# Openings of two large attentions reordered, and the second router moved into its layer norm

## What is computed

```python
x = L0_attn_a(x)   # two-way Mamba
x = L0_ffn(x)      # depthwise conv, 8 experts, top 2
x = L0_attn_b(x)   # linear recurrence
x = L0_ffn(x)
x = L1_attn_a(x)   # 16 heads of 8, local window 128, plus 64-token latent attention, gated mix
x = L1_ffn(x)      # second layer norm, router, 8 experts, top 2, plus a shared expert
x = L1_attn_b(x)   # 16 heads of 8, rotary positions, causal
x = L1_ffn(x)
```

## Time and profile before

| | |
|---|---|
| median of 3 runs | 6284.84 us (6282.61 to 6287.77) |
| profiled execution, time | 6280.3 us |
| profiled execution, span | 6278.3 us |
| PE busy | 5075.5 us (81%) |
| DVE busy | 4231.9 us (67%) |
| POOL busy | 3279.0 us (52%) |
| ACT busy | 3138.2 us (50%) |
| mean granted clock of PE | 0.899 |

### The profile page before, as it was taken

The page is one execution under the profiler, slowest core; times in us unless marked ns, Lnnn a source line. Parts: engine busy times, 40 slices in busy tenths (PEclk is TensorE's granted clock), DMA queues, the critical chain, the costliest instruction groups (busy, mean ns, idle before and its releaser), DMA issues. The chain is left out here.

```text
span 6278.3 us, 78842 instructions
## 1 busy us (share of the span) xinstructions
PE 5075.5 (81%) x21870; PEld 2565.6 (41%) x21934; DVE 4231.9 (67%) x6079; ACT 3138.2 (50%) x5353; POOL 3279.0 (52%) x2351
## 2 busy tenths in 40 slices
PE   4888888888887797778977999854897799964897
PEld 1333333333332343534433555422565344432664
DVE  4889889999988474044765888752675566652675
ACT  4656656655654454223544777721232477731232
POOL 2888888888886252012623444317333456527333
PEclk8999999999999897578988999966998899976998
DMA  1233322222221000000001333222454343302455
GB/s 71 83 118 135 127 75 89 82 75 88 82 75 67 0 0 0 0 0 0 0 6 47 91 87 88 53 82 74 154 189 153 75 95 97 90 1 76 160 188 173
DMA packets 203166, 494.21 MB, mean 79 GB/s; under 512 B 32448, under 2 KB 57664, under 8 KB 191424
## 3 DMA queue, kind: packets, MB, share of 16 engines
q1 hardware_dynamic: 184640, 452.25, 23.0%
q0 software_dynamic: 18176, 37.79, 1.7%
HBM read 381.79 MB, written 108.12 MB: 78 GB/s over the span
## 5 line engine op out<-in xcount | busy, mean ns | idle before, releaser
L360 POOL TENSOR_TENSOR mamba_bu<-mamba_du,mamba_b_all 128x1024 f32<-128x1024 f32 x512 | 1197.3, 2355 | 229.7 <-PE psum L454 172.3
L636 DVE TENSOR_TENSOR_SCAN mamba_bu<-psum,mamba_bu 128x512 f32<-128x512 f32 x1024 | 1189.6, 1205 | 132.7 <-POOL mamba_bu L360 88.6
L454 PE MATMUL psum<-mamba_bu,consts 128*128 128x512 f32 x2048 | 976.4, 600 | 6.1 <-DVE mamba_bu L642 1.5
L568 ACT ACTIVATE psum<-mamba_delta,A 128x510 f32<-128x510 f32 x1024 | 690.8, 685 | 545.8 <-DVE mamba_bu L636 524.2
L1754 ACT ACTIVATE ffn_moe_act<-ffn_moe_act 128x512 f32<-128x512 f32 x344 | 216.9, 631 | 721.2 <-DVE ffn_moe_act L1798 721.1
L642 DVE TENSOR_TENSOR mamba_bu<-mamba_bu,psum 128x1024 f32<-128x1024 f32 x448 | 536.8, 1198 | 58.4 <-remote 51.5
L1639 POOL DMA_INDIRECT results<-ffn_moe_y_rows,ffn_moe_row_of x312 | 302.2, 969 | 506.9 <-DVE ffn_moe_y_rows L1829 431.4
L454 PEld LDWEIGHTS psum<-mamba_bu,consts 128*128 128x128 f32 x2048 | 396.3, 194 | 332.6 <-issue 318.4
L2187 POOL TENSOR_TENSOR loc_q_bd<-loc_q_max,weights_l1a 128x512 fp32r<-128x512 f32 x256 | 274.8, 1103 | 389.6 <-DVE loc_q_max L2431 374.2
L2422 DVE TENSOR_REDUCE cau_top<-psum 128x2 f32<-128x512 f32 (+1 forms) x384 | 263.1, 692 | 181.3 <-PE psum L2254 167.5
L2187 POOL TENSOR_TENSOR cau_q_bd<-cau_q_max,weights_l1b 128x512 fp32r<-128x512 f32 x256 | 258.5, 1044 | 241.2 <-DVE cau_q_max L2431 177.5
(11 more groups left out here) (410 smaller groups left out, 11290.2 us busy)
## 6 DMA issues: line engine op xcount, KB each, us to landing
mamba_b_all<-b_rows SPq DMA_DIRECT2D x256, 512.0 KB
ffn_moe_w_gu<-gate_up_parts SPq DMA_DIRECT2D x78, 1024.0 KB, 4.8
pairs<-empty_rows SPq DMA_DIRECT2D x6, 3432.0 KB, 13.1
ffn_moe_got<-pairs SPq DMA_DIRECT2D x78, 264.0 KB, 3.2
ffn_moe_w_down<-in_l_moe SPq DMA_DIRECT2D x78, 256.0 KB, 2.9
mamba_c_rows<-b_rows SPq DMA_DIRECT2D x32, 512.0 KB, 4.1
qk_rows<-loc_qk SPq DMA_DIRECT2D x16, 1024.0 KB, 7.5
ffn_moe_back<-results SPq DMA_DIRECT2D x32, 512.0 KB, 4.8
```

Of the source, the lines that this page charges most:

```text
L360: nc.gpsimd.tensor_tensor(bu[:, J % BU, :, :], du[:, q % 2, :, :], b, ALU.mult).then_inc(bu_ready, 1)
L454: last = nc.tensor.matmul(ysum[:, h, :], mem.ident, bu[:, J % BU, h, :], start=False, stop=(n == NST - 1), skip_group_check=True)
L568: nc.scalar.activation(by_seq(dA[i % DECAYS])[:, :, 1:S], by_seq(delta[:, q % 2, h, :])[:, :, 1:S], ACT.Exp, scale=mem.A[:, q % 2, h * NST ...
L636: nc.vector.tensor_tensor_scan(bu[:, J % BU, h, :], dA[i % DECAYS], bu[:, J % BU, h, :], 0.0, ALU.mult, ALU.add).then_inc(scanned, 1)
```

## The change

Four things in the attentions. The projections of tile 0 get banks of their own (bank_of: the position of the name in the list of inputs, so banks 0 and 1, or 0 to 3), and only the others claim work. Clearing is moved behind the parts of tile 0 and shared: ACT writes k_st after its two high parts, DVE clears the first k_bd buffer after its work on tile 0, POOL clears the second buffer, top and v after its own. The count is split into four semaphores. The first k_bd buffer is filled by DMAs from ACT's queue, ahead of ACT's high parts of tile 1.

In the norm: a new argument route. With it the loops are written out, PE multiplies U directly by the router's columns (logits), DVE copies the logits out, and l1_router is gone.

```diff
-        (mean_ready, ..., added, scaled) = ctx.enter_context(
+        (mean_ready, ..., added, scaled, shifted, logits_ready, logits_read) = ctx.enter_context(
...
+            def logits(t):
+                pe.wait_ge(shifted, t + 1 + LEAD)
+                pe.wait_ge(logits_read, t - 1 + LEAD)
+                for j in range(SUB):
+                    at = t * T + j * 128
+                    last = nc.tensor.matmul(mem.bank[4 + t % 2][:, j * NE:(j + 1) * NE], dst[:, at:at + 128], route[0], start=True, stop=True)
+                last.then_inc(logits_ready, 1)
+
+            def step(t, s):
+                mean(t + 2, s)
+                var(t, s)
+                if route is not None and t >= 2:
+                    logits(t - 2)
...
+            over_tiles(pe, NT - 2, step)
             var(NT - 2, 0)
             var(NT - 1, 1)
+            if route is not None:
+                for t in range(NT - 4, NT):
+                    logits(t)
...
+            def take_logits(t):
+                dve.wait_ge(logits_ready, t + 1 + LEAD)
+                dve.sem_inc(PASSED[0], 1)
+                nc.vector.tensor_copy(route[1][:, t * SUB:(t + 1) * SUB, :],
+                                      mem.bank[4 + t % 2][:, 0:SUB * NE].rearrange("p (j e) -> p j e", j=SUB)).then_inc(logits_read, 1)
+
+            def step(t, s):
+                center(t + 2, s)
+                scale(t, s)
+                if route is not None and t >= 3:
+                    take_logits(t - 3)
...
             scale(NT - 2, 0)
             scale(NT - 1, 1)
+            if route is not None:
+                for t in range(NT - 5, NT):
+                    take_logits(t)
...
-            l1_router(nc, stage + "_route", mem, U, logits)
...
+        def bank_of(use):
+
+            return mem.bank[inputs.index(use[0])] if use[0] in inputs and use[1] == 0 else work
...
             store_rows(0)
-            sp.wait_ge(zeroed, 6 + LEAD)
+            sp.wait_ge(st_cleared, 1 + LEAD)
             spread_queries(0)
-            spread_diagonal(0)
+            sp.wait_ge(kst_cleared, 2 + LEAD)
             spread_keys(0)
+            sp.wait_ge(bd_cleared, 2 + LEAD)
             spread_diagonal(1)
...
+            def clear_rest():
+                nc.gpsimd.memset(k_bd[:, 1, :, :, :].bitcast(F32), 0.0).then_inc(bd_cleared, 1)
+                nc.gpsimd.memset(top[:, :, :], 0.0).then_inc(cleared, 1)
+                nc.gpsimd.memset(v[:, :, :], 1.0).then_inc(cleared, 1)
...
             def claim(use):
-                pe.wait_ge(work_read, position[use] + LEAD)
+                if bank_of(use) is work:
+                    pe.wait_ge(work_read, position[use] + LEAD)
...
+            high("q", 0)
+            high("k", 0)
             for a in range(2):
-                nc.scalar.activation(k_st[:, a, :, :], ...).then_inc(zeroed, 1)
-            for tile in range(2):
-                high("q", tile)
-                high("k", tile)
+                nc.scalar.activation(k_st[:, a, :, :], ...).then_inc(kst_cleared, 1)
+            act.wait_ge(rows_stored, 16 + LEAD)
+            act.wait_ge(bd_cleared, 2 + LEAD)
+            for i in range(GH):
+                for part in range(PARTS):
...
+                    act.dma_start(k_bd[at:at + HD, 0, :, i, :].bitcast(F32), rows).then_inc(bd_landed[0], 16)
+            high("q", 1)
+            high("k", 1)
...
-            nc.vector.memset(k_bd[:, :, :, :, :].bitcast(F32), 0.0).then_inc(zeroed, 1)
-            if mix is not None:
-                mix.clear(dve)
             for tile in range(2):
...
+                if tile == 0:
+                    nc.vector.memset(k_bd[:, 0, :, :, :].bitcast(F32), 0.0).then_inc(bd_cleared, 1)
+                    if mix is not None:
+                        mix.clear(dve)
-            dve.wait_ge(zeroed, 6 + LEAD)
+            dve.wait_ge(cleared, 2 + LEAD)
             take_v(0)
```

More of the change, by code:

```diff
@@ L58, in tile_pairs, with layer_norm @@
             step(pair * 2 + slot, slot)
-def layer_norm(nc, stage, mem, src, dst, affine=None, twice=False, residual=None):
+def layer_norm(nc, stage, mem, src, dst, affine=None, twice=False, residual=None, route=None):
     with ExitStack() as ctx:
@@ L75, in layer_norm, with over_tiles @@
         ps_var = [mem.bank[2], mem.bank[3]]
-        (mean_ready, centered, squared, var_ready, log_done, rstd_ready, added, scaled) = ctx.enter_context(
-            signals(nc, stage, "mean", "centered", "squared", "var", "log", "rstd", "added", "scaled"))
+        (mean_ready, centered, squared, var_ready, log_done, rstd_ready, added, scaled, shifted, logits_ready, logits_read) = ctx.enter_context(
+            signals(nc, stage, "mean", "centered", "squared", "var", "log", "rstd", "added", "scaled", "shifted", "logits", "logits_read"))
         block = ctx.enter_context(nc.Block())
         n_log = 2 if residual is not None else 1
+        def over_tiles(eng, last, step):
+            if route is None:
+                with eng.Fori(0, last // 2) as pair:
+                    for slot in range(2):
+                        step(pair * 2 + slot, slot)
+            else:
+                for t in range(last):
+                    step(t, t % 2)
         @block.tensor
@@ L139, in square @@
                 nc.gpsimd.tensor_tensor(sq[:, s, :], dst[:, cols(t)], dst[:, cols(t)], ALU.mult).then_inc(squared, 1)
-            tile_pairs(pool, square)
+            over_tiles(pool, NT, square)
         @block.scalar
@@ L1275 @@
 LIMIT = 10.0
[L1278 to L1310, removed]
 BLK = 512
@@ L2189, in diagonal @@
                 last.then_inc(q_bd_ready, 1)
-            if rope:
-                for tile in range(2):
+            for tile in range(2):
+                if rope:
                     for a in range(2):
@@ L2196, in _ @@
                         low_rope(a, tile)
+                if tile == 0:
+                    clear_rest()
             for s in range(STEPS_A):
@@ L2222, in project @@
                 else:
-                    nc.tensor.matmul(work, w[name], U[:, columns(tile)], start=True, stop=True, skip_group_check=True).then_inc(work_ready, 1)
+                    nc.tensor.matmul(bank_of(use), w[name], U[:, columns(tile)], start=True, stop=True, skip_group_check=True).then_inc(work_ready, 1)
             def out(s):
```

39 lines of the change are left out of this document (16 added, 23 removed).

## The result

| | before | changed |
|---|---|---|
| median of the compared runs, us | 6286.3 (4 runs, 6282.6 to 6288.4) | 6228.8 (4 runs, 6227.5 to 6233.9) |
| profiled execution, us | 6280.3 (span 6278.3) | 6229.6 (span 6227.6) |

The ratio is 0.9911, 95% interval [0.9894, 0.9928]: 57.5 us won by the medians (predicted: 63, at 6222). A second comparison on another chip gave 0.9912 [0.9898, 0.9925], 6225.5 against 6282.1. The profiled pair shows only 50.7, because the profiled execution of before lay 6 us under its median. The table is worked out from start times in the timelines: a norm from its first product to the first routing operation; an opening from GpSimd's first clearing to the first scores.

What follows compares the result with a forecast made beforehand. No engine bounds the whole span, so gains were read by stage: 43.6 (routers) + 9.0 + 11.2 (attention openings) - 1.1 (signals) = 62.7 us, 6280.3 to 6217.6; median 4.5 higher: 6222 us. Range of 8 in 10: 6208 to 6241.

Steps and rivals of the forecast that it cites:

- rival B: Less is won: TensorE in its order or ScalarE's issues become the bound, or the opening is absorbed; say 6240 us; 15%.
- Router, what falls away and the end: Each router: 31.7 us removed, 1.6 kept as way to the next stage, 5.9 added behind the last shift.
- 11 x 0.22 = 2.4 us, and a tile of 2.66: Inside the norm: VectorE gets 11 copies at 0.22 us each in a full chain, making its tile 2.66 us.
- level, so TensorE adds nothing: Norm: TensorE's two products and eight narrow ones take 2.71 us a tile against VectorE's 2.66, adding no time.
- a tile near 3 us with TensorE never idle: Norm: sign of a wrong forecast; at worst the eight narrow products cost 1.71 us, making 3.61 a tile.
- Rival C: Slower: narrow products pull the clock down through the whole norm, 3.15 us more a tile, 88 us, 6310; 3%.
- First opening, 9.0: First attention: store to DRAM at 3393.6 instead of 3402.59, 9.0 us sooner, with landing to scores kept at 12.9.
- stays: Attention openings: landing to first scores keeps its length, 12.9 us in the first and 15.2 in the second.
- Second opening, 11.2: Second attention: last rotation starts 11.5 us sooner, POOL's stretched instructions cost 0.3, so 11.2 us won.
- The second queue at 0: Attention loads: issuing the first k_bd from ScalarE's queue shortens landing to scores by 0.
- the rival's price: More is won: norm's end stays warm (2 x 2.7), second queue brings its own engines (2 x 3.7); 6209 us; 10%.
- Signals, 1.1: Three more in each of nine norms and each attention, 33 with two events of 17 ns: 1.1 us lost.

## Why the prediction was right, and where it was off

The forecast's mechanism held: both routers left the path, the first store came as soon as said and the second 1 us after its time, and the total, 6228.8 for 6222, lies inside the range and on the side of rival B. That it came so close is in part luck: by the stages the change won 50.7 us in the traced pair, 12 short of the 62.7 of the sum, and the medians show 57.5, chiefly because the traced execution of before was 6 us under its median. By its own terms:

- **Router, what falls away and the end** (31.7, 1.6, 5.9): measured 5.4 and 5.8 for the two tails, 1.64 for the transition. Right, the price at clock 0.50 too.
- **"11 x 0.22 = 2.4 us, and a tile of 2.66"**, with "level, so TensorE adds nothing": this is the term that failed. For the 2.4 stand 7.8 us in the first norm and 7.1 in the second, at a tile of 2.97: 10.1 too little, which with 0.6 won back in the tails makes the 9.6 us that the two norms fall short. The amounts of work were right or on the high side: without the wait the norm was only 1.4 us longer than before and its tile 2.61, with VectorE's share of it 2.54. What was missing is the wait. The prediction saw at the norm's end that the product of tile 13 waits for the copy of tile 11, and did not carry this wait into the steady part, where mean and variance stand behind it, nor to the start, where no bank is free for the third tile. It was named as a sign ("a tile near 3 us with TensorE never idle"); it came with TensorE idle, for the cause was not its amount of work.
- **Rival C**, the narrow products pulling the clock down: not so. The clock fell to 0.50 for some us behind the pause, and stayed at 1.00 with the same products and no pause. But its price, a slow stretch inside the norm, was paid in small: 3.8 us at most. Rival B's heading, TensorE in its order as the bound, is what happened, but not by its price (products of 1.71).
- **First opening, 9.0**: the store's part is exact; 1.6 was lost between landing and scores. The 12.9 of the term was a low draw: with before's attention code the distance was 12.9, 14.1 and 14.6 in three traces, mean 13.9. But that isn't all. With the changed code it was 15.7 on the mean of eight traces (12.6 to 16.8), 1.8 more, and in the second attention 14.9 against 13.9. So "stays" is probably wrong by 1 to 2 us for each, though the traces with before's code are few; neither the old queue and order nor holding the keys' rows back made it shorter, and the cause stays open. On these means the opening went from 32.5 to 25.5, 7 us.
- **Second opening, 11.2**: 11.9 in the pair, 10.4 on the same means (40.0 and 29.7). That the pair is so near is two errors of opposite sign. The loads took 13.7 us instead of 15.2. The projections took 6.7 us at clock 0.55, where the prediction let the fourth run at the higher level. In five of these eight traces it did, with the store 10.1 to 10.3 us after the start of the stage, and in three it did not, with 11.4 or 11.5. So this, too, is a draw.
- **The second queue at 0**: right. Of the page cited (the Trainium skill, DMA: Bandwidth & Descriptors, Issuing engines are not separate DMA queues) the traces agree with the first half: the DMA share from landing to scores is 0.50 to 0.53 with two queues and 0.50 to 0.52 with one. The second half, that issue time is saved, agrees too (4 us of SyncE's, above) but was worth nothing that shows here. In the rival's price, 394 KB at 102 GB/s are 3.9 us, not 3.7.
- **Signals, 1.1**: the sum left out that the two routers' three signals each go. The trace has 27 more events of 17 ns where the term had 66, so 0.5 us. The stretches outside the four stages lost 2.6 us in the pair, and their own spread is larger.

## What to carry to other kernels

When work is hung into a pipeline, follow each new wait through the order of the engine that makes it: what stands behind it there, and does that lead back to what it waits for? The round divided by the number of buffers is a lower bound on the tile, whatever the busy times say; more buffers or an earlier consumer cut it (here one 0.18 us copy moved ahead of the scale won to the last shift what two PSUM banks did). And price a wait on TensorE twice: the wait, and the slower products that may follow it.

## What the runs showed of the hardware that was not expected

- A pause of 1.62 us of TensorE, after 14 us of nearly full use, was followed, from some 1.5 us behind its end, by 9 us at granted clocks of 0.60, 0.50 and 0.76, with TensorE busy throughout. The slow stretch cost twice what the pause did (3.8 and 1.8 us). Twelve norms of six traces have this pause and a lower clock behind it; in two of them it was over within 5 us of the pause's end and cost 2.3 and 2.5.
- The same spread loads, to eight partitions each, ran at 78 to 120 GB/s from one execution to the next at a DMA share of 0.50 to 0.53. Landing to scores took 12.2 to 17.2 us over all traces. What sets the rate in an execution isn't known from these runs.
